# A four-layer kernel on one core: the balancing of the second batch's mixing matrices is moved to GpSimd, beside that of the first on DVE

## What is computed

```python
def sinkhorn_log(logits, num_iters=50, tau=0.1):
    Z = logits / tau
    def step(carry, _):
        u, v = carry
        u = -logsumexp(Z + v[..., None, :], axis=-1)
        v = -logsumexp(Z + u[..., :, None], axis=-2)
        return ((u, v), None)
    (u, v), _ = scan(step, (u0, v0), None, length=num_iters)
    return exp(Z + u[..., :, None] + v[..., None, :])
...
H_res = sinkhorn_log(H_res_logits)
H_pre = softmax(H_pre_logits); H_post = softmax(H_post_logits)
g = sigmoid(gate)[0]
H_res = (1.0 - g) * I + g * H_res
x_pre = einsum('btnc,btn->btc', x_streams, H_pre)
y = x_pre @ W_branch
x_mixed = einsum('btij,btjc->btic', H_res, x_streams)
y_distributed = einsum('btc,btn->btnc', y, H_post)
return x_mixed + y_distributed
```

## Time and profile before

| | us |
|---|---|
| time of three runs | 1584.46, 1589.5, 1593.9 (median 1589.5) |
| the profiled execution | 1587.23 |
| its span, first to last instruction | 1585.5 |
| PE busy in the span | 1080.2 (68%) |
| DVE busy | 829.8 (52%) |
| ACT busy | 561.1 (35%) |
| POOL busy | 337.0 (21%) |
| mean granted clock of TensorE, of full speed | 0.847 |

### The profile page before, as it was taken

The page is one execution under the profiler, slowest core; times in us unless marked ns, Lnnn a source line. Parts: engine busy times, 40 slices in busy tenths (PEclk is TensorE's granted clock), DMA queues, the critical chain, the costliest instruction groups (busy, mean ns, idle before and its releaser), DMA issues. The chain is left out here.

```text
span 1585.5 us, 21544 instructions
## 1 busy us (share of the span) xinstructions
PE 1080.2 (68%) x7522; PEld 466.3 (29%) x7522; DVE 829.8 (52%) x1718; ACT 561.1 (35%) x736; POOL 337.0 (21%) x439
## 2 busy tenths in 40 slices
PE   3789877999897747740011567777873980889777
PEld 2333333444343432330001211111241440333343
DVE  4387732222112433279976397777137461877334
ACT  2156661333200304340042236666614000466602
POOL 2323321454300401100055200000002671133200
PEclk9779997999999879965555859999985995799998
DMA  3500002112001250020000411000003134421001
GB/s 107 147 14 22 12 1 80 60 60 80 1 0 44 63 120 1 1 75 0 0 1 0 142 32 30 17 16 1 1 0 116 33 115 113 68 42 22 1 0 53
DMA packets 50147, 67.05 MB, mean 42 GB/s; under 512 B 6077, under 2 KB 40369, under 8 KB 50061
## 3 DMA queue, kind: packets, MB, share of 16 engines
q1 hardware_dynamic: 47816, 60.77, 14.2%
q0 software_dynamic: 2256, 5.26, 1.1%
HBM read 46.93 MB, written 18.82 MB: 41 GB/s over the span
## 5 line engine op out<-in xcount | busy, mean ns | idle before, releaser
L667 DVE TENSOR_REDUCE a2a_mx<-a2a_ring 128x2 f32<-128x1024 f32 x128 | 150.9, 1219 | 47.5 <-PE a2a_ring L535 47.0
L75 PE MATMUL f_pp<-xt,f_wgu 128*128 128x512 f16 x672 | 150.0, 384 | 3.5 <-POOL f_wgu L1102 3.5
L623 ACT ACTIVATE a2a_pr<-a2a_ring 128x1024 f32<-128x1024 f32 x128 | 129.5, 1024 | 61.3 <-PE a2a_ring L567 61.0
L667 DVE TENSOR_REDUCE a3a_mx<-a3a_ring 128x2 f32<-128x768 f32 (+3 forms) x88 | 96.2, 1123 | 33.0 <-PE a3a_ring L535 31.7
L667 DVE TENSOR_REDUCE a0a_mx<-a0a_ring 128x2 f32<-128x768 f32 (+3 forms) x88 | 96.1, 1122 | 29.8 <-PE a0a_ring L535 28.4
L175 POOL TENSOR_TENSOR p_w<-s_w,p_w 128x544 f16<-128x544 f32 (+2 forms) x6 | 15.2, 2549 | 452.9 <-ACT p_w L197 452.9
L623 ACT ACTIVATE a0a_pr<-a0a_ring 128x1024 f32<-128x1024 f32 x80 | 81.0, 1023 | 42.4 <-PE a0a_ring L567 42.0
L623 ACT ACTIVATE a3a_pr<-a3a_ring 128x1024 f32<-128x1024 f32 x80 | 81.1, 1023 | 42.3 <-PE a3a_ring L567 42.0
L75 PEld LDWEIGHTS f_pp<-xt,f_wgu 128*128 128x128 f16 x672 | 65.4, 99 | 85.5 <-issue 6.8
L183 PE MATMUL n_pt<-ident,s_xn 128*128 128x128 f32 x96 | 17.7, 369 | 100.6 <-DVE s_xn L158 100.6
L1076 DVE TENSOR_TENSOR f_sd<-f_sd,f_pp 128x512 f32<-128x512 f32 x28 | 19.2, 687 | 122.3 <-ACT f_sd L1091 122.3
(11 more groups left out here) (278 smaller groups left out, 2030.5 us busy)
## 6 DMA issues: line engine op xcount, KB each, us to landing
stack_scratch<-p_qk SPq DMA_DIRECT2D x126, 128.0 KB
f_ws<-in_L_gu SPq DMA_DIRECT2D x14, 512.0 KB
f_ws<-in_L_down SPq DMA_DIRECT2D x14, 256.0 KB
a0a_qs<-stack_scratch SPq DMA_DIRECT2D x16, 192.0 KB, 3.5
a2a_qs<-stack_scratch SPq DMA_DIRECT2D x16, 192.0 KB, 3.8
s_w<-in_L_w SPq DMA_DIRECT2D x4, 768.0 KB, 5.8
a3a_qs<-stack_scratch SPq DMA_DIRECT2D x16, 192.0 KB, 5.0
a3a_ks<-stack_scratch SPq DMA_DIRECT2D x16, 192.0 KB, 5.3
```

The costliest lines, as they stand in the source:

```text
L75: mm = pe.matmul(out, left(a, c), right(b, c), start=first and k == 0, stop=last and k == n - 1)
L623: act.activation(pr[:, og % 2, u, :, 0:width], ring[:, f % 3, :, 0:width], ACT.Exp, scale=a.scale).then_inc(exped, 1)
L667: dve.tensor_reduce(mx[:, n % 2, i, :, p0:p0 + heads], ring[:, k.max_fill[m] % 3, :, 0:heads * keys].rearrange("q h (p k) -> q h p k", k=k ...
```

## The change

POOL gets a program in the block "hs". It sets a tile of minus ones, waits for the exponential of `mix`, and balances the matrices of the second batch in a loop of 50 passes with eight steps each: pairs of row elements are added into a new tile `half_sums` (128x32), the pairs are added to the row sums (128x16), the sums are raised to the power of minus one (128x16, two tensors: sums and minus ones), the rows are multiplied (128x64, the inverse repeated four times), and the same four for the columns. Each step waits for the one before by a semaphore of POOL's own, `pool_balanced`.

DVE's loop keeps the same six steps for the first batch alone, each waiting for the one before. After its loop DVE waits for all of POOL's 400 steps, ahead of `binary.scales`. Nothing else changes.

```diff
--- before.py
+++ after.py
@@ -1131,8 +1131,10 @@
                 nc.sbuf_tensor("h_m2", [P, NT, 2], F32) as m2, \
                 nc.sbuf_tensor("h_i2", [P, NT * 2], F32) as i2, \
                 nc.sbuf_tensor("h_gt", [P, 3], F32) as gt, \
-                Phase(nc, "hs", "made squared meaned rooted centred exped gate_exped done balanced") as (
-                block, made, squared, meaned, rooted, centred, exped, gate_exped, done, balanced):
+                nc.sbuf_tensor("h_half", [P, NI, 2 * n], F32) as half_sums, \
+                nc.sbuf_tensor("h_minus", [P, NI * n], F32) as minus, \
+                Phase(nc, "hs", "made squared meaned rooted centred exped gate_exped done balanced pool_balanced minus_set") as (
+                block, made, squared, meaned, rooted, centred, exped, gate_exped, done, balanced, pool_balanced, minus_set):

             @block.sync
             def _(sp):
@@ -1158,6 +1160,39 @@
                 act.activation(mix[:, :, :], mix[:, :, :], ACT.Exp, scale=inv_tau).then_inc(exped, 1)
                 act.activation(pp[:, :, :], pp[:, :, :], ACT.Exp).then_inc(exped, 1)
                 binary.signs(act)
+
+            @block.gpsimd
+            def _(pool):
+                pool.memset(minus[:, :], -1.0).then_inc(minus_set, 1)
+                pool.wait_ge(minus_set, 1)
+                pool.wait_ge(exped, 1)
+                byrow = mix[:, NI:NT, :].rearrange("p t (i j) -> p (t i) j", j=n)
+                bycol = mix[:, NI:NT, :].rearrange("p t (i j) -> p t j i", j=n)
+                sums = m4[:, NI * n:NT * n]
+                pairs = half_sums[:, :, :]
+                byrow_pairs = pairs.rearrange("p t (i j) -> p (t i) j", j=2)
+                bycol_pairs = pairs.rearrange("p t (i j) -> p t j i", j=n)
+                inverse = i4[:, NI * n:NT * n]
+                with pool.Fori(0, iters) as it:
+                    pool.tensor_tensor(byrow_pairs, byrow[:, :, 0:2], byrow[:, :, 2:4], ALU.add).then_inc(pool_balanced, 1)
+                    pool.wait_ge(pool_balanced, it * 8 + 1)
+                    pool.tensor_tensor(sums, byrow_pairs[:, :, 0], byrow_pairs[:, :, 1], ALU.add).then_inc(pool_balanced, 1)
+                    pool.wait_ge(pool_balanced, it * 8 + 2)
+                    pool.tensor_tensor(inverse, sums, minus[:, :], ALU.pow).then_inc(pool_balanced, 1)
+                    pool.wait_ge(pool_balanced, it * 8 + 3)
+                    pool.tensor_tensor(byrow, byrow, inverse.unsqueeze(2).to_broadcast([P, NI * n, n]),
+                                       ALU.mult).then_inc(pool_balanced, 1)
+                    pool.wait_ge(pool_balanced, it * 8 + 4)
+                    pool.tensor_tensor(bycol_pairs, bycol[:, :, :, 0:2], bycol[:, :, :, 2:4], ALU.add).then_inc(pool_balanced, 1)
+                    pool.wait_ge(pool_balanced, it * 8 + 5)
+                    pool.tensor_tensor(sums.rearrange("p (t j) -> p t j", j=n), bycol_pairs[:, :, :, 0],
+                                       bycol_pairs[:, :, :, 1], ALU.add).then_inc(pool_balanced, 1)
+                    pool.wait_ge(pool_balanced, it * 8 + 6)
+                    pool.tensor_tensor(inverse, sums, minus[:, :], ALU.pow).then_inc(pool_balanced, 1)
+                    pool.wait_ge(pool_balanced, it * 8 + 7)
+                    pool.tensor_tensor(bycol, bycol, inverse.rearrange("p (t j) -> p t j", j=n).unsqueeze(3)
+                                       .to_broadcast([P, NI, n, n]), ALU.mult).then_inc(pool_balanced, 1)
+                    pool.wait_ge(pool_balanced, it * 8 + 8)

             @block.vector
             def _(dve):
@@ -1197,31 +1232,25 @@

-                dve.sem_inc(balanced, 2)
                 with dve.Fori(0, iters) as it:
-                    for k in range(6):
-                        for half in range(2):
-                            tiles = slice(half * NI, (half + 1) * NI)
-                            own = slice(half * NI * n, (half + 1) * NI * n)
-
-                            dve.wait_ge(balanced, it * 12 + (2 * k + half + 1))
-                            byrow = mix[:, tiles, :].rearrange("p t (i j) -> p (t i) j", j=n)
-                            bycol = mix[:, tiles, :].rearrange("p t (i j) -> p t j i", j=n)
-                            sums, inverse = m4[:, own], i4[:, own]
-                            if k == 0:
-                                op = dve.tensor_reduce(sums, byrow, AX.X, ALU.add)
-                            elif k == 3:
-                                op = dve.tensor_reduce(sums.rearrange("p (t j) -> p t j", j=n), bycol, AX.X, ALU.add)
-                            elif k == 2:
-                                op = dve.tensor_tensor(byrow, byrow, inverse.unsqueeze(2).to_broadcast([P, NI * n, n]),
-                                                       ALU.mult)
-                            elif k == 5:
-                                op = dve.tensor_tensor(bycol, bycol, inverse.rearrange("p (t j) -> p t j", j=n)
-                                                       .unsqueeze(3).to_broadcast([P, NI, n, n]), ALU.mult)
-                            else:
-                                op = dve.reciprocal(inverse, sums)
-                            op.then_inc(balanced, 1)
-                dve.wait_ge(balanced, 12 * iters + 2)
+                    byrow = mix[:, 0:NI, :].rearrange("p t (i j) -> p (t i) j", j=n)
+                    bycol = mix[:, 0:NI, :].rearrange("p t (i j) -> p t j i", j=n)
+                    sums, inverse = m4[:, 0:NI * n], i4[:, 0:NI * n]
+                    dve.tensor_reduce(sums, byrow, AX.X, ALU.add).then_inc(balanced, 1)
+                    dve.wait_ge(balanced, it * 6 + 1)
+                    dve.reciprocal(inverse, sums).then_inc(balanced, 1)
+                    dve.wait_ge(balanced, it * 6 + 2)
+                    dve.tensor_tensor(byrow, byrow, inverse.unsqueeze(2).to_broadcast([P, NI * n, n]),
+                                      ALU.mult).then_inc(balanced, 1)
+                    dve.wait_ge(balanced, it * 6 + 3)
+                    dve.tensor_reduce(sums.rearrange("p (t j) -> p t j", j=n), bycol, AX.X, ALU.add).then_inc(balanced, 1)
+                    dve.wait_ge(balanced, it * 6 + 4)
+                    dve.reciprocal(inverse, sums).then_inc(balanced, 1)
+                    dve.wait_ge(balanced, it * 6 + 5)
+                    dve.tensor_tensor(bycol, bycol, inverse.rearrange("p (t j) -> p t j", j=n).unsqueeze(3)
+                                      .to_broadcast([P, NI, n, n]), ALU.mult).then_inc(balanced, 1)
+                    dve.wait_ge(balanced, it * 6 + 6)
+                dve.wait_ge(pool_balanced, 8 * iters)
                 binary.scales(dve)

                 dve.wait_ge(gate_exped, 1)
```

## The result

The changed kernel takes 1910.2 us in the median of four runs (1908.05 to 1914.23), against 1587.24 before (four runs); the ratio is 1.203, 95% interval 1.1983 to 1.2077. It is slower by a fifth. The prediction was 1755, between 1645 and 1965: right in direction and inside the range, 155 us short of the middle.

A forecast was written before the change was run, and what follows sets the result against it. DVE's balancing loop, 97 us without cover, was taken as the bound; POOL's 50 passes of 5.25 us (262.5) plus 5 for holding up would end at 953.4, +169 on 1587.2 giving 1756, predicted as 1755, range 1645 to 1965.

The forecast's parts named there:

- That POOL would set the end: Balancing loop: POOL done at 953.4 us, bw_cols waits for it, everything behind only moves, +169 us.
- the price of the power: POOL's two powers a pass: 27 passes over the elements guessed, 0.9 us each on top of a plain step.
- the power is dearer: Rival: POOL's power costs three times the estimate, a pass 8.85 us, +349, 1936 us; chance 0.20.
- powers near 1.1 us: Sign in POOL's loop: the prediction is wrong if powers are not near this; each 0.1 us moves the time 10 us.
- The plain steps from two rows: POOL's sums and multiplications: fixed 179 ns plus 2.11 ns an element, giving 0.213 us for 16 elements, 0.247 for 32.
- the charge for a repeated operand: POOL's two multiplications a pass: 0.99 ns more for each element, so 0.377 us in place of 0.314.
- The wait of a dependent POOL step: Between POOL's eight steps: 0.15 us each, the middle of 0.08, 0.145 and 0.25; 1.20 us a pass.
- DVE's half: DVE's loop on the first batch alone: 1.83 us a pass, 91.5 us in place of 97, at most 5.5 gained.
- not slower: Rival: POOL's steps so short that DVE's loop ends last, 5.5 us earlier, 1582 us; chance 0.02.
- Holding each other up: POOL beside DVE's loop: 0.25 us lost in each of 18 passes, 5 us; at most 24 us.
- The rival of loops in turn: Rival: POOL's and DVE's loops hold each other up until they run in turn, +257, 1844 us; chance 0.04.
- The clock: PE's clock behind the loop is already at the lower level, 0.50, so longer idle time takes nothing more from it.

The follow-up runs named there:

- the run with single steps: The kernel before plus single POOL powers and products of several sizes, on tiles of their own, beside DVE's balancing loop; 1586.25 us.
- the run with the wait moved: DVE balancing the first batch alone, without POOL's program, the wait for a pass's last step moved to the top of the next pass; 1581.62 us.
- The two runs on DVE alone: The changed kernel without POOL's program and the wait for it, 1595.6 us; the same with the pass's last wait moved to the next pass's top, 1581.62 us.
- the run with a free power: The changed kernel with POOL's two powers a pass replaced by plain products of the same shape, second batch's reciprocals left out; 1638.03 us.

## Why the prediction was right or wrong, point by point

**That POOL would set the end, and that nothing covers it: right.** DVE's 315.1 us of waiting and bw_cols 0.03 us after POOL's last step (1106.09 + 0.33 to 1106.45) show it. What lies behind only moved.

**The size: wrong, by the price of the power.** In us a pass:

| term | predicted | measured |
|---|---|---|
| the six plain steps | 1.67 | 1.61 |
| two powers | 2.23 | 5.82 |
| waits between steps and the loop's boundary | 1.35 | 0.92 |
| sum | 5.25 | 8.35 |

The failed step is the price of the power, an estimate of mine from the plain slope: 27 passes over the elements, 0.9 us on top of a plain step. It measured 2.91 - 0.22 = 2.69 us on top, three times as much, which I had as the upper end and as the rival "the power is dearer", 1936 us with a chance of 0.20. By the prediction's own sign, powers near 1.1 us, it was wrong. POOL's loop ended at 1106.4 in place of 953.4, 153 us late: some 179 by the powers (3.59 us in 50 passes) and 3 by the later start, less 21 by the waits and the boundary, 3 by the plain steps and 5 by the hold, which were all put too dear. With the right power alone the sum gives the rival's 1936, 26 above the measured time; those smaller errors happen to go the other way. The rows before the change hold no power, and the 158 ns an element could not be read from them; guessing passes was no more than guessing. The bounds on both sides did their work, the choice between them had no ground.

**The plain steps from two rows: right.** 0.213 for 16 elements against 0.216 and 0.222; 0.247 for 32 against 0.240 where the elements of a pair are neighbours, but 0.303 for the columns; the multiplications 0.298 and 0.326 against 0.377, so the charge for a repeated operand that I took from L880 does not hold here: without a repeated operand a product of this size took 0.318 (the run with single steps). The page named in the prediction (the Trainium skill's GPSIMD Engine Reference, section 7) has the column steps dearer for their 16-byte step. In sum the trace agrees, 0.091 a pass and 4.6 us in all where my estimate from it was 5, but step by step it does not. The addition of 32 elements is 0.063 us dearer than on rows (0.303 - 0.240) where half again of 2.11 ns an element, the same estimate, gives 0.034, and the multiplication of 64 is 0.028 dearer (0.326 - 0.298) where it gives 0.068. The two misses cancel.

**The wait of a dependent POOL step: too dear.** Of the three rows it was the smallest, 0.08 us, and not the middle. It stood in the row whose operands were closest in size. The boundary of 0.38, 0.15 in my sum, gave part of that back.

**DVE's half: wrong, but hidden.** I had 91.5 us and 5.5 to gain, it takes 102 (689.3 to 791.3), 5 more than both halves together before. The 0.035 and the lengths were right (1.66 us from 0.22, 0.25, 0.22, 0.26, 0.25, 0.27 with their gaps); the boundary was 0.38 and not 0.19. I had added the lengths of three sequencer instructions, 0.15 us, and some 0.2 us more that have no row of their own; the run with the wait moved hides them behind the last step. So my rival "not slower" had no case at all: had POOL been free of cost, the end of this code would still have come 5 us later. The two runs on DVE alone show both, the cost and its removal: with the wait moved the half takes 88.0 us.

**Holding each other up: a mechanism of the right kind, but too dear.** Beside DVE's loop a POOL pass took (789.38 - 688.49) / 12 = 8.41 us, after it 8.35, so the twelve passes lost 0.7 us and not 5. I had spread eight steps evenly over the pass, while in 70% of it POOL is inside a power and starts nothing. That is only a part of it: with plain steps only (the run with a free power) a POOL pass took 3.00 us beside DVE's loop ((791.91 - 686.89) / 35) and 2.96 after it, 0.04 lost and not 0.25. DVE lost 0.06 us a pass there ((790.6 - 687.7) / 49 = 2.10 against 2.04), 3 us in all, visible as a multiplication of 0.33 us at 702.83 where a POOL step runs from 702.78.

The power holds nothing up and is not held (2937 ns at the longest, 2911 in the median). Of DVE's 100 multiplications in the changed kernel 64 lie wholly inside a power, and none of these takes more than 0.27 us; in order of time, the first two:

```profile
689.10 2.94 POOL L1181 TENSOR_TENSOR h_i<-h_m,h_minus 128x16 f32<-128x16 f32 x1
689.88 0.23 DVE L1243 TENSOR_TENSOR h_mix<-h_mix,h_i 128x64 f32<-128x64 f32 x1
...
690.72 0.27 DVE L1250 TENSOR_TENSOR h_mix<-h_mix,h_i 128x64 f32<-128x64 f32 x1
```

Four of the 100 take more than 0.30 us, and each of them starts within 0.1 us behind the start of a plain POOL step. The longest of them is 423 ns where 269 is the median, the longest of POOL's plain steps 392 where 303 is: none is held for longer than one plain instruction of the other engine. DVE's sums and reciprocals, which read one tensor, are not held: at the longest 266 and 254 ns. The Trainium skill's SBUF — State Buffer, section "Who interferes with whom", has a DVE instruction with two SBUF inputs contend and the pair of ports locked for one instruction; by that, the trace agrees for the plain steps and not for the power, beside which DVE's two-input steps run as if alone. The rival of loops in turn falls with it.

**The clock: right.** It is 0.51 in the stretch, and what follows has the same granted clock as before, 0.83, and keeps its length (800.15 us against 801.5).

## What to carry to other kernels

Two chains that already cover each other's latency on one engine gain little by being parted: each then pays its own waits, and the loop's boundary too. Here half the work alone took DVE 88.0 us with its best boundary, and both halves interleaved and written out 89.4. Before an operation goes to another engine for want of the right one there, measure that one instruction in two sizes beside something that hides it; here this would have taken one run. In a loop of small dependent steps put the wait for the last step at the top of the next pass, or write passes out; both were tried on DVE alone.

## What the runs showed of the hardware

- A power on POOL is 158 ns an element a partition over some 0.40 us (16 to 64 elements, exponent -1). Exponents 2 and 0.5 and a base of 0.001 in place of 3 give the same within 40 ns at 16 elements. A product is 2.1 ns an element over 0.19 us.
- DVE's multiplications run through a power of POOL unhindered (64 of them, none above 0.27 us). Plain POOL steps of 0.2 to 0.3 us can hold one up by 0.15 to 0.17 us (423 ns against 269; 440 against 271 in the run with a free power).
- The two loops whose body ends in a wait for its last instruction cost 0.38 us of idle time a turn, on DVE as on POOL. The sequencer's own instructions sum to 0.15 us on DVE and to 0.11 on POOL (29, 32 and 45 ns). With the wait after the branch it is 0.11 us on DVE. In the loop with two chains the boundary has 0.08 us of idle time, and 0.18 (1.6 in nine) when five passes are written out; why was not tried.
- A step that waits for the one before follows after 0.08 us on POOL and after 0.03 to 0.04 on DVE.
